# SmoothQuant stage of a gated transformer stack: x shifted on ScalarE, turned as f32, side jobs re-placed

## What is computed

```
def _smooth_quant_linear(x, w):          # x [T, D], w [O, D]
    s = sqrt(max(amax_x, EPS) / max(amax_w, EPS))    # per column
    xs, ws = x / s, w * s
    x_scale = max(rowmax(|xs|), EPS) / 127
    w_scale = max(rowmax(|ws|), EPS) / 127
    x_q, w_q = round(xs / x_scale), round(ws / w_scale)
    return x_q @ w_q.T * x_scale * w_scale.T
h = _smooth_quant_linear(layernorm(x), gate_up_weight)   # 512 -> 512
a = silu(h[:, :256]) * h[:, 256:]
x = x + tanh(g) * _smooth_quant_linear(a, down_weight)   # 256 -> 512
```

## Time and profile before

| what | value |
|---|---|
| median of 3 runs (lowest to highest) | 1400.78 us (1399.51 to 1404.86) |
| profiled execution, its own time | 1398.27 us |
| its span, first to last instruction | 1396.6 us |
| TensorE, VectorE, ScalarE, GpSimd busy | 83%, 62%, 47%, 30% of the span |
| first stage | from 0 to about 234.7 us |
| mean granted clock of TensorE | 0.93 |

### The profile page before, as it was taken

How to read it: one execution, slowest core, us unless ns; L and a number is a source line. 1 busy time by engine, 2 the same in 40 slices (tenths; PEclk the granted TensorE clock), 3 DMA queues, 4 the chain that set the end, 5 groups by cost and what they waited for, 6 DMA issues and landing times. The chain is left out here.

```text
span 1396.6 us, 16561 instructions
## 1 busy us (share of the span) xinstructions
PE 1165.5 (83%) x5256; PEld 504.7 (36%) x5317; DVE 860.0 (62%) x1325; ACT 654.6 (47%) x1147; POOL 413.2 (30%) x479
## 2 busy tenths in 40 slices
PE   5775875999799999963459988998999999876897
PEld 3443432555444444431013222222322222223453
DVE  7899875214245555315798887778777777226543
ACT  2554452555322222241347666556655556724543
POOL 3475470010132222113334432222222220015332
PEclk8987898999989999985669999999999999996999
DMA  7223123444244444337813332322222220017011
GB/s 262 88 103 121 53 98 135 153 138 150 87 159 146 150 143 149 115 110 228 188 50 104 89 107 68 89 80 86 71 85 85 74 74 2 3 10 84 35 38 46
DMA packets 106356, 141.58 MB, mean 101 GB/s; under 512 B 20788, under 2 KB 75572, under 8 KB 106280
## 3 DMA queue, kind: packets, MB, share of 16 engines
q1 hardware_dynamic: 87432, 111.37, 25.0%
q0 software_dynamic: 18368, 28.85, 8.0%
q10 hardware_dynamic: 480, 0.39, 0.1%
HBM read 97.44 MB, written 46.27 MB: 103 GB/s over the span
## 5 line engine op out<-in xcount | busy, mean ns | idle before, releaser
L2394 DVE TENSOR_REDUCE a_top<-PS 128x2 f32<-128x1024 f32 x256 | 308.4, 1222 | 94.8 <-PE PS L2155 90.8
L2241 ACT ACTIVATE a_E<-PS 128x512 f32<-128x512 f32 x512 | 277.7, 596 | 150.0 <-PE PS L2138 149.8
L2138 PE MATMUL PS<-a_Q,a_K 99*128 99x512 bf16 (+1 forms) x469 | 157.0, 386 | 16.6 <-ACT a_E L2241 6.2
L2155 PE MATMUL PS<-a_K,a_Q 64*128 64x512 bf16 x512 | 104.2, 405 | 48.9 <-DVE a_top L2394 29.6
L1367 PE MATMUL PS<-f_W,f_GT 128*128 x312 | 141.6, 597 | 0.0
L2168 PE MATMUL PS<-a_E,a_V 128*32 128x512 f32 x1024 | 136.9, 607 | 0.4 <-ACT a_E L2241 0.4
L2138 PEld LDWEIGHTS PS<-a_Q,a_K 99*128 99x128 bf16 (+1 forms) x512 | 44.2, 97 | 155.4 <-ACT a_E L2241 105.4
L1771 POOL TENSOR_TENSOR a_qf<-a_qf,a_tab 128x512 f32<-128x512 f32 x15 | 19.1, 1270 | 269.3 <-DVE a_swapped L2338 269.3
L1423 DVE TENSOR_TENSOR f_H<-f_SG,PS 128x256 f32<-128x256 f32 x39 | 16.4, 421 | 125.2 <-ACT f_SG L1407 125.2
L1367 PEld LDWEIGHTS PS<-f_W,f_GT 128*128 128x128 f32 x312 | 56.9, 192 | 57.2 <-issue 57.2
L2155 PEld LDWEIGHTS PS<-a_K,a_Q 64*128 64x128 bf16 x512 | 24.7, 93 | 141.9 <-issue 72.4
(11 more groups left out here) (361 smaller groups left out, 2006.2 us busy)
## 6 DMA issues: line engine op xcount, KB each, us to landing
f0r_raw<-in_L_ffn_W_dram SPq DMA_DIRECT2D x24, 512.0 KB, 4.6
a_K<-k_parts SPq DMA_DIRECT2D x192, 64.0 KB, 2.3
a_Q<-a_q_parts SPq DMA_DIRECT2D x186, 64.0 KB, 2.4
f_y<-f_Y SPq DMA_DIRECT2D x39, 256.0 KB, 2.0
v_units<-V SPq DMA_DIRECT2D x16, 512.0 KB, 2.8
a_V<-v_units SPq DMA_DIRECT2D x16, 512.0 KB, 3.8
k_parts<-f_k_parts SPq DMA_DIRECT2D x16, 384.0 KB, 3.4
a_q_parts<-a_parts SPq DMA_DIRECT2D x16, 384.0 KB, 2.8
```

Source lines behind the costliest of these rows:

```text
L2138: nc.tensor.matmul(PS[:, 4 + h % 2, :], K6[k][0:rows_, o, head // 2, kt * P:(kt + 1) * P], Q6[k][0:rows_, o, head // 2, :], start=True, st ...
L2155: last = nc.tensor.matmul(PS[:, 2 * pair + o, :], Q6[k][at, o, h // 2, t * P:(t + 1) * P], K6[k][at, o, h // 2, :], start=True, stop=True)
L2241: nc.scalar.activation(E[step % 2][:, h, :], PS[:, 4 + h % 2, :], ACT.Exp).then_inc(exp_done, 1)
L2394: nc.vector.tensor_reduce(top[:, h - h % 2:h - h % 2 + 2, t], PS[:, 2 * pair:2 * pair + 2, :], AX.X, ALU.max).then_inc(maxed, 1)
```

## The change

- VectorE no longer quantizes. ScalarE shifts x as well as w (`shift_x`). TensorE turns the shifted f32 values (`turn_shifted`), against the f32 identity. The constant is subtracted in the copies out of PSUM, which write bf16: by ScalarE for up's w (two halves) and all of down, by VectorE for up's x (`take_up_x`, two halves). The arrays `xq` and `wq` go.
- TensorE's turns go in halves with waits between: up's w into banks 2, 3 and 0, 1, then up's x into the same banks once ScalarE has emptied them; down's w into 4, 5, its x into 4, 6. TensorE's turns of down stand ahead of up's products, as before.
- Layer norm statistics of batches 1 to 3 are all taken in pass 0, with one root; later passes only normalize.
- The side jobs have six slots with counts of their own in each pass (`FILL`). Slot 0 moves ahead of the turns of x; slot 3 stands between the weight-scale rows of up and down; in the last pass the first slots are empty, its products use banks 0 to 3 and stand ahead of the last slot.
- The last pass is written out behind the loop.

```diff
-            def turn_quantized(L, q, bank, done):
-                for c in range(L.kc):
+            def turn_shifted(q, half, banks, done):
+                for c in range(2 * half, 2 * half + 2):
                     for t in range(4):
-                        o = PS[:, bank + c // 2, (c % 2) * 256 + t * 64:(c % 2) * 256 + (t + 1) * 64].bitcast(BF16)
-                        last = nc.tensor.transpose(o, q[:, t, c * P:(c + 1) * P], identb[:])
+                        last = nc.tensor.transpose(PS[:, banks[c % 2], t * P:(t + 1) * P], q[:, t, c * P:(c + 1) * P], identf[:])
                 last.then_inc(done, 1)
...
+            def finish_up(u):
+                pe.wait_ge(up.w_shifted, u + 1)
+                turn_shifted(up.ws, 0, (2, 3), up.wqT_done)
+                pe.wait_ge(up.wsc_row_ready, u + 1)
+                pe.wait_ge(up.x_scaled, u + 1)
+                turn_shifted(up.ws, 1, (0, 1), up.wqT_done)
+                pe.wait_ge(up.x_shifted, u + 1)
+                for half, banks in ((0, (2, 3)), (1, (0, 1))):
+                    pe.wait_ge(up.wqT_ready, 2 * u + half + 1)
+                    turn_shifted(up.xs, half, banks, up.xqT_done)
+            def finish_down(d):
+                pe.wait_ge(down.w_shifted, d + 1)
+                pe.wait_ge(down.wsc_row_ready, d + 1)
+                turn_shifted(down.ws, 0, (4, 5), down.wqT_done)
+                pe.wait_ge(down.x_shifted, d + 1)
+                pe.wait_ge(down.wqT_ready, d + 1)
+                turn_shifted(down.xs, 0, (4, 6), down.xqT_done)
...
+                side.tensor(pe, i, 0)
+                pe.wait_ge(up.x_ready, u + 1)
+                for half in range(2):
+                    pe.wait_ge(up.reduced, 4 * u + half + 1)
+                    turn_x(up, u, half, 2 * half)
...
+                s_rows(up, u, (0, 0), (1, 0))
+                side.tensor(pe, i, 1)
                 if d >= 0:
                     s_rows(down, d, (6, 0), (6, 256))
-                side.tensor(pe, i, 1)
-                if u < NB:
-                    wsc_row(up, u, 1)
                 side.tensor(pe, i, 2)
+                wsc_row(up, u, 1)
+                side.tensor(pe, i, 3)
...
-                if u < NB:
-                    pe.wait_ge(up.wq_ready, u + 1)
-                    turn_quantized(up, up.wq, 2, up.wqT_done)
-                    pe.wait_ge(up.wsc_row_ready, u + 1)
-                    pe.wait_ge(up.xq_ready, u + 1)
-                    turn_quantized(up, up.xq, 0, up.xqT_done)
-                side.tensor(pe, i, 3)
+                finish_up(u)
+                side.tensor(pe, i, 4)
                 if d >= 0:
-                    pe.wait_ge(down.wq_ready, d + 1)
-                    turn_quantized(down, down.wq, 5, down.wqT_done)
-                    pe.wait_ge(down.xq_ready, d + 1)
-                    turn_quantized(down, down.xq, 6, down.xqT_done)
-                if u < NB:
-                    pe.wait_ge(up.wqT_ready, u + 1)
-                    pe.wait_ge(up.xqT_ready, u + 1)
-                    for t in range(TB):
-                        product(up, t, t)
+                    finish_down(d)
+                pe.wait_ge(up.xqT_ready, 2 * u + 2)
+                for t in range(TB):
+                    product(up, t, t)
                 if d >= 0:
-                    pe.wait_ge(down.wsc_row_ready, d + 1)
-                    pe.wait_ge(down.wqT_ready, d + 1)
                     pe.wait_ge(down.xqT_ready, d + 1)
                     for t in range(TB - 1):
                         product(down, t, DOWN_AT[t])
-                side.tensor(pe, i, 4)
+                side.tensor(pe, i, 5)
                 if d >= 0:
                     pe.wait_ge(y_ready, d * TB + 1)
                     product(down, TB - 1, DOWN_AT[TB - 1])
...
+            wsc_row(down, d, 4)
+            side.tensor(pe, NB, 3)
+            finish_down(d)
+            side.tensor(pe, NB, 4)
+            pe.wait_ge(down.xqT_ready, NB)
+            for t in range(TB):
+                product(down, t, t)
+            side.tensor(pe, NB, 5)
...
+            def shift_x(L, b):
+                act.wait_ge(L.x_scaled, b + 1)
+                for t in range(4):
+                    last = nc.scalar.activation(L.xs[:, t, :], L.xs[:, t, :], ACT.Copy, bias=ROUNDER,
+                                                scale=L.inv_scale[:, t:t + 1])
+                last.then_inc(L.x_shifted, 1)
+            def take_up_w(u):
+                for half, bank in ((0, 2), (1, 0)):
+                    act.wait_ge(up.wqT_done, 2 * u + half + 1)
+                    nc.scalar.activation(up.wqT[:, 2 * half:2 * half + 2, :], PS[:, bank:bank + 2, :], ACT.Copy,
+                                         bias=-ROUNDER).then_inc(up.wqT_ready, 1)
+            def take_down_w(d):
+                act.wait_ge(down.wqT_done, d + 1)
+                nc.scalar.activation(down.wqT[:], PS[:, 4:6, :], ACT.Copy, bias=-ROUNDER).then_inc(down.wqT_ready, 1)
+            def take_down_x(d):
+                act.wait_ge(down.xqT_done, d + 1)
+                nc.scalar.activation(down.xqT[:], PS[:, 4:7:2, :], ACT.Copy, bias=-ROUNDER).then_inc(down.xqT_ready, 1)
...
+                side.scalar(act, i, 0)
+                root(up, u)
...
                 side.scalar(act, i, 1)
-                if u < NB:
-                    shift_w(up, u)
-                    take_wsc_row(up, u, 1)
                 side.scalar(act, i, 2)
+                shift_w(up, u)
+                take_wsc_row(up, u, 1)
+                side.scalar(act, i, 3)
+                shift_x(up, u)
+                take_up_w(u)
                 if d >= 0:
                     shift_w(down, d)
                     take_wsc_row(down, d, 4)
-                if u < NB:
-                    take_turned(up, u, up.wqT, 2, up.wqT_done, up.wqT_ready)
-                    take_turned(up, u, up.xqT, 0, up.xqT_done, up.xqT_ready)
-                side.scalar(act, i, 3)
+                    shift_x(down, d)
+                side.scalar(act, i, 4)
                 if d >= 0:
-                    take_turned(down, d, down.wqT, 5, down.wqT_done, down.wqT_ready)
-                    take_turned(down, d, down.xqT, 6, down.xqT_done, down.xqT_ready)
-                if u < NB - 1:
-                    norm_root(u + 1)
+                    take_down_w(d)
+                    take_down_x(d)
...
+            side.scalar(act, NB, 3)
+            shift_x(down, d)
+            take_down_w(d)
+            take_down_x(d)
             side.scalar(act, NB, 4)
+            side.scalar(act, NB, 5)
...
+            def take_up_x(b):
+                for half, bank in ((0, 2), (1, 0)):
+                    v.wait_ge(up.xqT_done, 2 * b + half + 1)
+                    nc.vector.tensor_scalar(up.xqT[:, 2 * half:2 * half + 2, :], PS[:, bank:bank + 2, :], ROUNDER, None,
+                                            ALU.subtract).then_inc(up.xqT_ready, 1)
 
...
-                if u < NB:
-                    quantize_w(up, u)
-                    quantize_x(up, u)
-                if d >= 0:
                     x_scales(down, d, 6, 0)
                     if d == 0:
                         v.wait_ge(tg_ready, 1)
                     gate_scale(d)
-                    quantize_w(down, d)
-                    quantize_x(down, d)
+                if u == 0:
+                    v.wait_ge(x_loaded[1], 16)
+                    row_stats(range(TB, NB * TB))
+                take_up_x(u)
+                if u == 0:
+                    row_roots(2, slice(TB, NB * TB))
                 if u < NB - 1:
-                    if u == 0:
-                        v.wait_ge(x_loaded[1], 16)
-                    row_stats(u + 1)
                     normalize(u + 1)
-                if u < NB:
-                    take_up(u)
+                take_up(u)
                 if d >= 0:
-                    take_down(d, d == NB - 1)
+                    take_down(d, False)
...
-    IN_SLOT = (1, 0, 3, 2, 2)
+    FILL = (0, 1, 1, 3, 2, 2), (1, 1, 1, 2, 1, 2), (1, 1, 1, 2, 1, 2), (1, 1, 1, 2, 1, 2), (0, 0, 0, 3, 2, 2)
...
-        for b, kind, n in [job for slot in (self.schedule[i][:2], self.schedule[i][2:])[half] for job in slot]:
+        for b, kind, n in [job for slot in (self.schedule[i][:3], self.schedule[i][3:])[half] for job in slot]:
```

More of the change, by code:

```diff
@@ new lines, in finish_down, with turn_down_x @@
+            def finish_down(d):
[5 more added lines that the diff above has]
+                turn_shifted(down.xs, 0, (4, 6), down.xqT_done)
+            def turn_down_x(d):
+                pe.wait_ge(down.reduced, 2 * d + 1)
+                pe.wait_ge(down.x_ready, (d + 1) * TB)
+                turn_x(down, d, 0, 4)
@@ L311, in _ @@
+            for i in range(NB):
+                u, d = i, i - 1
+                pe.wait_ge(up.w_loaded, 16 * (u + 1))
+                for half in range(2):
+                    if u:
+                        pe.wait_ge(hs_ready, (u - 1) * TB + 2 * half + 2)
```

(43 more changed lines are left out.)

122 lines of the change are left out of this document (54 added, 68 removed).

## The result

The changed kernel takes 1409.72 us (median of 11 runs, 1405.13 to 1411.74), the kernel before 1401.17 (11 runs): the ratio is 1.0052, 95% interval 1.0040 to 1.0064. Forecast was 1406.5, range 1388 to 1416. The change costs some 7 us by the ratio (8.6 by the medians), and its interval holds the bound of 0.5%. Slower by a little was the likeliest case of the forecast, and the size lies in the upper part of that case's own range, 1401 to 1412. The profiled execution, the fastest of the eleven, took 1405.13, its span 1403.4, 6.8 more than before.

What follows compares the result with a forecast made beforehand. The prediction took a TensorE and ScalarE chain close beside VectorE as the bound; its pass and clock terms summed to +5.9 us, 1404.2 for the profiled execution, 1406.5 forecast as the median, range 1388 to 1416.

Steps and rivals of the forecast that it cites:

- Slower by a little: Whole kernel: the forecast's own case, chance 0.5, range 1401 to 1412 us; 0.22 of it slower by more than 7 us.
- What bounds the kernel: First stage: one chain over TensorE and ScalarE runs close beside VectorE and sets what VectorE's relief is worth.
- VectorE's relief: VectorE loses quantization and statistics, gains two PSUM copies: net 11.3 us less in passes 1 and 2, 7.3 in pass 3.
- Slot 0: Passes 1 to 3: a job ahead of x's turns makes a new VectorE stall of 1.35 us, three times.
- From the products on: Pass 2: from the products' start to the next pass's first reduction, 11.0 us instead of 10.4.
- Pass 1: Products start 35.0 us into the pass instead of 38.5; length 46.0 us for 48.94, -2.9.
- Pass 2: Products start 36.2 us into the pass against 40.25; length 47.2 us for 51.06, -3.9.
- Pass 3: v2 and v3 in slot 3 cost 2.7 us more than two x jobs; length 48.1 for 47.35, +0.8.
- Pass 0: Nine side jobs instead of eight form the chain, statistics hidden, products at 46 us; +3.9 us with a low clock.
- Last pass: Seven side jobs remain once down's scales come, none done before; the final store comes late, +5.6 us.
- Clock: Low TensorE clock after waits in passes 2, 3 and last: bounds 0 and 1.7 us each, half taken, +2.4 us.
- The second rival: Clock low in over half the stretch from x's scales to the products: slower, 1413 to 1424 us, chance 0.15.

Runs made afterwards that it cites:

- The two loads: Changed kernel with superfluous work in passes 1 to 3: four bn_stats on VectorE, ratio to the kernel before 1.0068; or four copies on ScalarE, ratio 1.0136.
- tail back: Changed kernel with the last pass's seven side jobs placed as in the kernel before; ratio to the kernel before 1.0024.
- keep clock: Changed kernel with superfluous TensorE matmuls ahead of the turn of a, ten in passes 1 to 3, fourteen in the last; ratio to the kernel before 1.0043.
- r behind: Changed kernel with the angles job r behind the other job of slot 1 instead of ahead of it; ratio to the kernel before 1.0070.

## Why the prediction was right, and where it was off

- *What bounds the kernel.* Right: a chain over TensorE and ScalarE, with VectorE's total beside it. The two loads show it from both sides. It is not ScalarE's queue alone: with the x shift taken off it, TensorE's turns behind VectorE's scales of down come next.
- *VectorE's relief.* 11.3 us said, 8.4 and 7.5 measured in passes 1 and 2. The copies out of PSUM took 1.22 us each, as taken; left out was `xh`, 4.14 and 4.03 us instead of 2.23 and 2.33. What was relieved became waits (1.43 and 3.42 us ahead of `take_up_x`, 3.38 ahead of the last y). The idle time of 2 to 4 us ahead of `hs`, named as a sign, was 0.42 and 0.55 there.
- *Slot 0.* The stall was there, 0.92 us (1.35 said). That the move itself was a gain, some 7 us over the kernel, stood nowhere in the prediction.
- *From the products on.* 11.0 us said, 10.4 measured in passes 1 and 2 (10.4 and 10.8 before the change).
- *Pass 1.* Products 34.7 us into it, 35.0 said; -3.8 for -2.9. In tail back, the same code took 47.00: -1.9.
- *Pass 2.* -2.8 for -3.9, products at 37.8 for 36.2. The failed term is r and the job behind it: "2.7 to 2.8 each", measured 3.78 on TensorE each. In tail back, with r at 2.06, the pass took 47.03: -4.0. Which pass pays for the low clock differs between executions, so no pass by itself confirms its term. That the pass before started from a wait for a store (6.56 us, in its chain) is not in the prediction.
- *Pass 3.* +2.5 for +0.8, by the same two jobs (both 3.78).
- *Pass 0.* +5.2 for +3.9: r took 3.77, x's turns 3.45 for 16 (2.1 said), so the products started at 48.90, not 46.0. The statistics were hidden, as said; the root behind them waited for ScalarE's jobs, 3.98 us, and delayed nothing: TensorE ended the pass.
- *Last pass.* +7.3 for +5.6: the first job took 3.62. The tail's placement is 5.2 of the 7.3.
- *Clock.* The mis-sized term: half of a bound was taken, +2.4 over three passes. Passes 0, 2, 3 and the last are 5.8 beyond their own terms together (1.3, 1.1, 1.7, 1.7), and pass 1 is 0.9 better. The sum was +5.9, the stage measured +8.4. That the whole execution came within 1 us of the forecast (1405.13 for 1404.2) is luck in part: the rest of the kernel, which no term touches, gave 1.6 back.
- *The second rival.* By its own condition it does not hold: from x's scales to the products the mean granted clock was 1.00, 0.90 and 0.91 in passes 1 to 3.
- *A slip.* The "55" among the forecast lengths is the time at which pass 0 was to end, 55.25; as a length it is 42. Measured: 44.43.
- *The page's rule on turns.* By TensorE: Matmul & The Clock Gate, Part 4: PE-mode transpose, of the Trainium skill, turns would not have raised the clock. This case's trace does not agree. In pass 2 TensorE did only turns between 124.6 and 135.2 us. The clock fell to 0.50 after a wait of 2.76 us, the 16 turns of up's w took 3.47 us from 129.71 on, and the 16 of up's x behind them 1.94 us, the full rate: the clock rose to 1.00 at about 133, during turns alone. In pass 0 the 16 turns of x took 3.45 us behind a wait of 2.38.

## What to carry to other kernels

A busy share of 94% does not say by itself that an engine is the bound: before moving its work away, find what ends its idle time at the end of the loop, and put a known load on each engine in turn, at more than one place of its queue. Work put on a half-idle engine can cost in full if it is queued between two waits of a chain; what fills a queue there (side jobs, a copy that waits for a store) should stand where the chain waits anyway, and the last pass of a pipelined loop needs such fillers most.

## What the runs showed of the hardware

- Behind f32 matmuls with one row (r) the clock was low: entered at 1.00, r took 2.06 us and the next job 3.60 us (keep clock, pass 2); entered at 0.50 it stayed there (3.78, then 3.78).
- The clock rose from 0.50 to 1.00 while TensorE did only turns (changed kernel, 129.7 to 133.5 us).
- A VectorE tensor_scalar of 128x512, f32 from SBUF, took 0.54 us, and 1.50 us where it met a tensor_tensor of GpSimd.
- Ten superfluous bf16 matmuls in a wait of 3 us cost nothing, and r behind them took 2.06 us in each of passes 1 to 3; passes 2 and 3 were 2.0 and 1.7 us shorter, less than the scatter of a pass. In the last pass fourteen of them, followed by waits of 2.56 and 3.05 us, gave nothing.
- Identical code over 42 us differed by 3.5 us between executions (42.29 and 45.75, the last pass of the changed kernel and of r behind) through the granted clock alone, mean 0.83 against 0.73: one k job took 3.75 us instead of 1.98, one v job 3.42 instead of 1.88.
